# Attention kernel: row sums of plain heads issued inside the next projection, the two banks of the row maxima exchanged, single row-maximum matmuls between score tiles

## The reference

```
h   = layernorm(x)                                  # no scale, no shift
qk  = h @ W_qk + b_qk -> q, k of 8 heads of 64      # v = h @ W_v + b_v
o   = softmax(q k^T / 8) v                          # per batch and head, 1024 x 1024 scores
x   = x + (layernorm(o @ W_out + b_out) * gamma + beta + h) / sqrt(2)
h2  = layernorm(x);  hp = h2 shifted by one token
out = x + sigmoid(mix_r(h2, hp) @ W_r^T) * (relu(mix_k(h2, hp) @ W_k^T)^2 @ W_v^T)
```

## Time and profile before

| | |
|---|---|
| median of 3 runs | 2723.48 us (2719.68 to 2723.65) |
| the profiled execution | 2721.03 us, its span 2719.2 us |
| busy share of the span | PE 97%, POOL 56%, DVE 60%, ACT 47% |
| granted TensorE clock, mean | 0.989 of full speed |

### The profile page before, as it was taken

How to read it: one execution, slowest core, us unless ns; L and a number is a source line. 1 busy time by engine, 2 the same in 40 slices (tenths; PEclk the granted TensorE clock), 3 DMA queues, 4 the chain that set the end, 5 groups by cost and what they waited for, 6 DMA issues and landing times. The chain is left out here.

```text
span 2719.2 us, 31997 instructions
## 1 busy us (share of the span) xinstructions
PE 2625.8 (97%) x11376; PEld 1782.0 (66%) x11376; DVE 1631.3 (60%) x2679; ACT 1290.6 (47%) x1833; POOL 1521.1 (56%) x819
## 2 busy tenths in 40 slices
PE   6999999999999999999999999999579999999999
PEld 5655656665565666556556666665358888888887
DVE  7555455456545545654554555455278787878785
ACT  3345346335534634553463455344245555555554
POOL 3576477567647756764775676577323333333333
PEclk9999999999999999999999999999779999999999
DMA  2222122122112212211221221122322222222220
GB/s 97 63 47 51 36 78 53 42 71 55 44 38 75 55 40 71 57 42 48 66 55 40 70 60 39 40 50 79 122 90 99 85 96 89 93 92 89 96 77 32
DMA packets 108410, 178.32 MB, mean 66 GB/s; under 512 B 22401, under 2 KB 22913, under 8 KB 108289
## 3 DMA queue, kind: packets, MB, share of 16 engines
q1 hardware_dynamic: 108288, 176.75, 22.5%
HBM read 92.02 MB, written 50.59 MB: 52 GB/s over the span
## 5 line engine op out<-in xcount | busy, mean ns | idle before, releaser
L417 DVE TENSOR_REDUCE half_max<-ps_max 128x1 f32<-128x512 f32 x1024 | 680.3, 687 | 549.7 <-PE ps_max L780 543.4
L324 POOL TENSOR_TENSOR acc<-acc,probs 128x1024 f32<-128x1024 f32 x384 | 914.0, 2380 | 157.5 <-ACT probs L623 109.2
L623 ACT ACTIVATE probs<-ps_st 128x1024 f32<-128x1024 f32 x512 | 522.0, 1023 | 591.8 <-PE ps_st L801 589.6
L812 PE MATMUL ps_o<-probs,v 128*64 128x512 f32 x2048 | 467.7, 598 | 0.0
L800 PE MATMUL ps_st<-qA,kA 128*128 128x512 f32 x1024 | 415.3, 406 | 13.9 <-DMA qB<-max_row 9.4
L801 PE MATMUL ps_st<-qB,kB 65*128 65x512 f32 x1024 | 408.2, 399 | 0.0
L780 PE MATMUL ps_max<-kA,qA 128*128 128x512 f32 x1024 | 386.8, 416 | 3.7 <-issue 1.4
L320 POOL TENSOR_TENSOR acc<-probs 128x1024 f32<-128x1024 f32 x64 | 152.8, 2387 | 287.6 <-ACT probs L623 287.6
L812 PEld LDWEIGHTS ps_o<-probs,v 128*64 128x64 f32 x2048 | 135.6, 136 | 265.4 <-issue 236.5
L780 PEld LDWEIGHTS ps_max<-kA,qA 128*128 128x128 f32 x1024 | 188.6, 188 | 138.6 <-issue 63.5
L800 PEld LDWEIGHTS ps_st<-qA,kA 128*128 128x128 f32 x1024 | 194.7, 190 | 82.3 <-ACT probs L623 32.7
(11 more groups left out here) (174 smaller groups left out, 4629.6 us busy)
## 6 DMA issues: line engine op xcount, KB each, us to landing
stage<-in_L_attn_x_dram SPq DMA_DIRECT2D x32, 512.0 KB, 5.8
qA<-qA SPq DMA_DIRECT2D x128, 128.0 KB, 2.3
kB<-kA SPq DMA_DIRECT2D x128, 128.0 KB, 2.4
o_hi_scratch<-spare SPq DMA_DIRECT2D x128, 128.0 KB, 2.3
o_lo_scratch<-oT SPq DMA_DIRECT2D x128, 128.0 KB, 2.4
o_hi<-o_hi_scratch SPq DMA_DIRECT2D x16, 1024.0 KB, 5.4
o_lo<-o_lo_scratch SPq DMA_DIRECT2D x16, 1024.0 KB, 7.7
xc<-in_L_attn_x_dram SPq DMA_DIRECT2D x16, 1024.0 KB, 5.2
```

Of the source, the lines that this page charges most:

```text
L324: pool.tensor_tensor(acc[:, :], acc[:, :], probs[:, j, :], ALU.add).then_inc(acc_done, 1)
L417: dve.tensor_reduce(half_max[:, r, kh:kh + 1], ps_max[(j + 1) % 2][:, :], AX_X, ALU.max).then_inc(max_done, 1)
L623: act.activation(probs[:, j, :], ps_st[j % 2][:, :], ACT.Exp).then_inc(exp_done, 1)
L812: ins = pe.matmul(ps_o[half * DH:(half + 1) * DH, :], v[:, j, hd * DH:(hd + 1) * DH], probs[:, j, half * HALF:(half + 1) * HALF], start=(j ...
```

## The change

On TensorE `plain_head` no longer issues `sum_rows` in `begin_head`; it issues it after 8 of the 12 matmuls of the projection's second half. The other heads keep theirs. Rj goes to bank j modulo 2 in place of (j+1) modulo 2, so R0 shares its bank with the turned maxima and R1 with the row sums; the waits of R0 and R1 are exchanged with it. The order of row matmuls and score tiles in a plain head becomes R1, S0, R2 R3, S1, R4, S2, R5, S3, R6, four projection matmuls, R7, S4. On ScalarE `store_sums` stands after `store_o` and `store_o_hi` in those heads. In `early_v_head` the turned x of tile 7 goes to `ps_max[1]` and waits for the copied sums.

```
-            bank = ps_misc if t in (4, 5, 6) else ps_max[1] if t in (1, 3) else ps_max[0]
+            bank = ps_misc if t in (4, 5, 6) else ps_max[1] if t in (1, 3, 7) else ps_max[0]
...
-                        dve.tensor_reduce(half_max[:, r, kh:kh + 1], ps_max[(j + 1) % 2][:, :], AX_X,
+                        dve.tensor_reduce(half_max[:, r, kh:kh + 1], ps_max[j % 2][:, :], AX_X,
...                                                                   # ScalarE, plain_head
                     if h >= 1:
-                        store_sums(b, h - 1)
+                        if h % HEADS == 0:
+                            store_sums(b, h - 1)
                         store_o(b, h - 1)
                     if h >= 2:
                         store_o_hi(b, h - 2)
+                    if h >= 1 and h % HEADS != 0:
+                        store_sums(b, h - 1)
...                                                                   # ScalarE, scaling_head
-                    store_sums(b, h - 1)
                     store_o(b, h - 1)
                     store_o_hi(b, h - 2)
+                    store_sums(b, h - 1)
...                                                                   # TensorE, rows
                         if j == 0:
                             pe.wait_ge(q_dup_in[0], 128 * b + 16 * h + 16)
                             pe.wait_ge(k_lo_done, 16 * b + 2 * h + 1)
-                            if h >= 2:
-                                pe.wait_ge(sum_copied, 8 * b + h - 1)
-                        if j == 1 and h >= 1:
-                            pe.wait_ge(max_row_done, 8 * b + h)
+                            if h >= 1:
+                                pe.wait_ge(max_row_done, 8 * b + h)
+                        if j == 1 and h >= 2:
+                            pe.wait_ge(sum_copied, 8 * b + h - 1)
...
-                        pe.matmul(ps_max[(j + 1) % 2][:, :], qA[h % 2][:, r * P:(r + 1) * P],
+                        pe.matmul(ps_max[j % 2][:, :], qA[h % 2][:, r * P:(r + 1) * P],
...
-                def begin_head(b, h):
+                def begin_head(b, h, sums_now=True):
                     if h >= 1:
                         p_at_v(b, h - 1, 4)
-                        sum_rows(b, h - 1, 8 * b + h + 1)
+                        if sums_now:
+                            sum_rows(b, h - 1, 8 * b + h + 1)
                     turn_max(b, h)

                 def plain_head(b, h, last):
-                    begin_head(b, h)
+                    begin_head(b, h, False)
                     free_of_qk(b, h + 1, 0)
                     project_qk(b, h + 1, 1, 0, 4)
                     rows(b, h + 1, 0, 1)
                     project_qk(b, h + 1, 1, 4, 8)
+                    if h >= 1:
+                        sum_rows(b, h - 1, 8 * b + h + 1)
+                    project_qk(b, h + 1, 1, 8, 12)
                     rows(b, h + 1, 1, 2)
-                    project_qk(b, h + 1, 1, 8, 12)
-                    rows(b, h + 1, 2, 3)
                     scores(b, h, 0, 1)
-                    rows(b, h + 1, 3, 4)
-                    scores(b, h, 1, 3)
-                    rows(b, h + 1, 4, 6)
+                    rows(b, h + 1, 2, 4)
+                    scores(b, h, 1, 2)
+                    rows(b, h + 1, 4, 5)
+                    scores(b, h, 2, 3)
+                    rows(b, h + 1, 5, 6)
                     scores(b, h, 3, 4)
-                    rows(b, h + 1, 6, 8)
+                    rows(b, h + 1, 6, 7)
                     more = not (last and h == HEADS - 2)
                     if more:
                         free_of_qk(b, h + 1, 1)
                         project_qk(b, h + 2, 0, 0, 4)
+                    rows(b, h + 1, 7, 8)
                     scores(b, h, 4, 5)
...                                                                   # TensorE, early_v_head
                     turn_xhat(b + 1, 6, turn_bank(6))
-                    pe.wait_ge(max_row_done, 8 * b + h + 1)
+                    pe.wait_ge(sum_copied, 8 * b + h)
                     turn_xhat(b + 1, 7, turn_bank(7))
```

## The result

The median went from 2723.57 us (six runs) to 2737.15 us (six runs), a ratio of 1.0056 (95% interval 1.0046 to 1.0067). The forecast was 2737. The profiled execution took 2735.74, its span 2734.0, 14.8 more than before. A hit so close is in part luck. One term was 5.7 us too small and two others together 5.1 too large, and 2737 itself was set between the sum on the profiled execution (2736) and the sum on the median (2738.5) without a working; the medians lie 13.6 apart where the sum was 15.0.

The account below looks back on a forecast made before the run. TensorE, busy 97% of the span, was taken to bound the kernel through distances between matmul starts. Terms 12.3+4.1+0.7-0.4-1.7 gave +15.0 us: 2736 on the profiled execution, 2738.5 on the median; forecast 2737, range 2722 to 2749.

Parts of the forecast that it names:

- R0's and S2's waits: TensorE, plain head: R0's wait for the copied sums (-0.25 us) and S2's for exponent 0 (-0.33) both go.
- The cost of the form: Sums between projection matmuls 8 and 9: switching matmul form both ways costs +0.34 us a plain head, bounds 0 and 0.5.
- The rival of a free form inside the projection: Sums inside the projection: the change of form costs nothing, total +1, 2722 to 2725 us; chance 0.10.
- The sums' longer way: Sums' DMAs before the reciprocal: hidden by 1 to 2 us; rival that they hold VectorE, 0.7 late giving 2765, chance 0.08.
- R1's wait: R1 now waits for the copied sums on ScalarE; load and signal just fit, taken as 0, up to 0.1 us.
- R4 costs 0, R5 costs 0.75: Plain-head row matmuls: R4 unhindered, R5 waits 0.65 for reduction 3 plus 0.10 behind a late load; bounds 0.4 and 1.0.
- The sums behind place 5 wait for GpSimd, +4.1: Turning head behind a place-5 head: its sums wait 0.58 us for GpSimd's later adds, seven times, +4.1.
- the last plain head: Its sums already waited for GpSimd, so it ends 0.98 us later: +0.7 over its 0.30.
- late heads: Place-0 heads keep their order and lose only R0's wait, seven times 0.25 us: -1.7.
- the two heads that used to be late for GpSimd: Two heads before the last plain head lost 0.4 us to late adds and lose it no more: -0.4.
- VectorE holds TensorE: R2 behind S0 delays reduction 2, then the stores and reduction 3, so R5 waits; forecast mechanism, slower, chance 0.70.

Follow-up runs that it names:

- e3: Kernel before with only the two banks exchanged (waits of R0 and R1 and tile 7 with them), sums and row order as before: 2709.78 us, ratio 0.9951.
- e1: Changed kernel with the row sums of plain heads, and ScalarE's copy of them, back at the head's beginning: 2724.60 us, ratio 1.0004.
- e8: Changed kernel with the row sums in fp32r with 128 columns of weights, two matmuls accumulating in one bank: 2701.02 us, ratio 0.9923.
- e11: Changed kernel with the row sums kept in float32 but with 128 columns of weights, accumulating in one bank: 2782.09 us, ratio 1.0219.
- e5: Changed kernel with R2 before S0 and VectorE's reduction 3 between the low parts of k and q: 2711.13 us, ratio 0.9966.
- e9: Changed kernel with R2 before S0, reduction 3 between the low parts of k and q, and sums in fp32r with 128 columns: 2672.97 us, ratio 0.9824.
- e2: Changed kernel with R2 issued before score tile S0 instead of behind it, sums still late: 2717.49 us, ratio 0.9977.
- e4: Changed kernel with VectorE taking reduction 3 between the low parts of k and q of half 1, not behind both: 2730.36 us, ratio 1.0026.

## Why the prediction was right, and where it wasn't

**R0's and S2's waits**: right. Both gone, as laid out; e3 gives the first by itself (0.26 for 0.25). S2 stands behind the late R4, which would hide a wait, but exponent 0 was done at T+6.82 (forecast T+6.86), before the T+6.90 at which S2 would have loaded.

**The cost of the form**: right in size (0.34 of the earlier trace rows, 0.35 in e1) and shown by e8 and e11 to be one of columns. The rival of a free form inside the projection is out.

**The sums' longer way**: hidden, as forecast. The reciprocal follows reduction 3 by 0.60 (419.07 to 419.67) and waits for nothing, so that rival is out too.

**R1's wait**: right. Load and signal fitted.

**R4 costs 0, R5 costs 0.75**: wrong as put. I took R4 to need only its bank. It also waits for the low part of k's second half, a wait that stood in `rows` at j == 4. In the old order that store was done at 414.63, 1.2 before R4 started, so it never showed; in my own layout it ran from T+6.52 to T+7.28, past R4's load at T+6.66. R4's load sat 0.84, R5's 0.37, where I had 0 and some 0.7. In sum the place of the wait makes little difference, since R5 starts only when VectorE's chain lets it: at T+8.85, where I had T+8.71. Those 0.14 are the mis-sized step. I had VectorE's next instruction 0.60 behind the start of reduction 2, as the reciprocal is behind reduction 3, but the store came 0.73 behind it (416.89 to 417.62), and in e5 and e9 a store again stands 0.72 behind a reduction. So the price is 0.87 for 0.75, the head +0.44 for +0.30, and 41 heads +18.0 for +12.3.

**The sums behind place 5 wait for GpSimd, +4.1**: wrong, by bookkeeping. I set the next head's beginning at T+26.3, an interval without the sums at its end, then took the sums' 0.95 off it. A place-5 head ends with them, at T+27.29, so TensorE reaches them at T+26.32. GpSimd was done at T+25.8, where I had put it. No wait: 0 for +4.1. The wait comes only in kernels with shorter plain heads, such as e5. The same slip stands in the last plain head: it grew by 0.97, as forecast, but 1.30 was already counted there (0.44 and the second sums), so it gives -0.3, not +0.7.

Put together from the trace: 41 x 0.44 = +18.0, late heads -1.8 (37.30 to 36.18, less the sums' 0.86), the two heads that used to be late for GpSimd -0.4, the last plain head -0.3: +15.5. The `turn_max` of the first and of the last head lie 1866.92 apart, where it was 1851.66: +15.3. My +15.0 was 5.7 short in one term and 5.1 too much in two others (4.1 and 1.0). That they cancel is luck.

**VectorE holds TensorE**: the mechanism that decided the sign, right. VectorE is busy 14.93 of 26.43 us, and the fixed order of its instructions made three of them late. e2 and e5 change only what stands in that chain and turn the sign; e4, which frees R5 alone, doesn't.

Open is why a store comes 0.72 to 0.73 behind a reduction and the reciprocal 0.60 behind it, and what late sums would give in the turning head, since no run has them there.

## What to carry to other kernels

When a matmul is moved, list all the waits that stand on it, not the one that is being moved: the one hidden so far comes next. Cost a chain by laying out the times of every engine in it, in order, and keep one definition of an interval for every head, or terms get counted twice. Keep matmuls of another column width side by side; each stretch of them among full-width ones cost 0.34 us here, both around `p_at_v` and inside the projection.

## What was not expected of the hardware

- The price of a change of form is in the columns alone: float32 between fp32r at 128 columns cost nothing beyond its own work (e11, 2.17 us for 2.18), float32 pairs of 64 columns cost 0.34.
- A late weight load costs about 0.1 us at the next matmul, even where its own matmul isn't held up: in the kernel before, R5's load came at 416.06, R5 started at 416.07, its own place (415.85 and 0.23), and the next matmul 0.32 behind it, at 416.39. R4 and R5 of the changed kernel pay the same 0.10 behind them, on top of the 0.57 and 0.10 by which they start late.
- Two full-width fp32r matmuls (0.47 us) do the work of four float32 half-width instructions (0.86 us and the change of form).
